# Statistics of x spread over fifteen steps, and three engines' programs unrolled twelve steps further

## The chip, the cores and the metric

The kernel runs on one core of a Trainium2 chip. The metric is the device time of one execution in microseconds (us). Engines: PE (TensorE: matmuls, with PEld for its weight loads), DVE (VectorE), ACT (ScalarE), POOL (GpSimd) and SP (SyncE), which here only issues DMAs. Each runs its own program in order; they meet at semaphores.

## The reference

One layer of cross attention and a mixture of experts behind it, 32 batches of 100 queries and 361 keys, width 256, 16 heads:

```
d  = layernorm(x)                                  # no gain, over 256 columns
q, k, v = d Wq + bq, ctx Wk + bk, ctx Wv + bv      # 16 heads of 16
z  = softmax(q k^T) v
x1 = x + layernorm(z + d) * gamma + beta
x2 = x1 + E(layernorm(x1)),  E(t) = t + sum over 2 of 8 experts of gate * ffn(layernorm(t))
```

What the change touches belongs to the first line: mean and variance of every row of x, from which come `rstd0` (one over the deviation) and `nb0` (minus the mean times it), one column for each batch.

## The kernel before

**Steps.** The attention is a software pipeline over the batches, one step for each, written as `iteration(turn, i)` for each engine. In step i, PE computes the row scores of batch i+1 (only for the row maxima, which DVE takes as `negmax`, L1390), the transposed scores of batch i, and the projections of batch i+3. Batches i-1, i-2 and i-3 are in the later stages: z is normalised, added and normalised again, and routed. A step has 12 slots (`s` in the code), and tables (`PLACE`, `START`, `TAIL`) say in which slot each operation stands. There are steps from -3 to 39; the experts' tiles follow and overlap with the last.

**Loops.** `pipeline(eng, iteration, first, last)` writes out the steps from -3 to 3*first-1, puts the steps from there to 26 into a loop of three steps a turn, and writes out the rest. PE and SP have `first=1`, so their loops begin at step 3; DVE, ACT and POOL have `first=2` and begin at step 6. In the loop a batch's number comes from a register; in written-out code it is a constant. What is special to one step (loads, statistics of x) can only stand in written-out code, behind `isinstance(turn, int)`.

**Statistics of x.** x is loaded in six parts, `X_LOADS`. Part 0 is issued by ACT, part 1 by SP at the start, part 2 by SP behind the first two key stacks, and parts 3, 4 and 5 (`X_LOAD_BEHIND`) by SP right behind the key stacks of batches 2, 3 and 4, that is in steps 0, 1 and 2. DVE takes a `bn_stats` for each batch (`x_sums`, L1330): batches 0 to 11 before step -1, and batches 12 to 31 five a step in steps 0 to 3, at the slots of `X_SUM_AT`. It waits for `x_loaded` at the first batch of each part. The sums are turned into deviations in four parts, `X_PARTS`: eight small operations on DVE (`x_variance_step`, L1340 to L1354), one a slot in slots 4 to 11 of steps 2 and 4 for the last two parts, then a power on POOL at the end of the same step (`inverse_deviation_x`, L694), and the offset on DVE at the end of the next (`x_offset`, L1363). ACT waits for `nb0_ready` before it normalises rows of a new part (steps 1 and 5, and in the loop).

**The key stack.** The keys of batch i+3 are split into three bfloat16 parts. ACT makes the high part and the middle one, POOL the rest (`k_rest`, L795) and the low part (`k_part`, L798, "the key part" below). SP waits for the low part and issues six DMAs of 192 KB (L660) that put the parts into `k_stack`, which lies in the tensor `stack_x`; PE's first row score of the batch, one step and some slots later, waits for them. Behind these SP issues a part of x where there is one, then the context of a later batch (`ct`, L635), then `zscr` (L645), by which z is laid out anew through DRAM; `z_in` (L639) reads it back, and POOL's `u` (L807) needs it. POOL's order in a step is: low part of the queries (L779), reciprocal deviation of the second norm (L788), `k_rest`, `u`, the key part, reciprocal deviation of the first norm (L810), and the rest.

**Guard.** `guard` (L1395) is DVE's cleaning of the exponentials `p_t`, four a step, at slots 0, 3, 6 and 9.

**Expert weights.** ACT issues 14 DMAs of 256 KB for `w1_s`, two in each turn of its loop, in the steps with i mod 3 of 0 and 1, at slot 5.

Of the kernel before, what the change touches and what calls it, by code (L numbers as in the profile page):

```python
# [12 lines left out]
B, Q, D = 32, 100, 256  # L13
# [14 lines left out]
FIRST = 4  # L28
X_LOADS = [slice(0, FIRST), slice(FIRST, 12), slice(12, 17), slice(17, 22), slice(22, 27), slice(27, B)]
X_LOAD_BEHIND = {1: 2, 2: 3, 3: 4, 4: 5}  # L30
X_SUM_AT = {(n // 5, (1, 4, 7, 9, 10)[n % 5]): 12 + n for n in range(20)}
TAIL_FROM = B - 3
X_PARTS = [slice(0, FIRST), slice(FIRST, 12), slice(12, 22), slice(22, B)]
SCORES_LAG, GUARD_LAG, VALUES_LAG = 3, 6, 9
# [112 lines left out]
def pipeline(eng, iteration, first=1, last=9):  # L147

    for i in range(-3, 3 * first):
        iteration(0, i)  # L150
    with eng.Fori(first, last) as turn:
        for r in range(3):
            iteration(turn, r)
    for i in range(3 * last, END):
        iteration(0, i)


def build(nc, x, ctx_t, wq_t, bq, wk_t, bk, wv_t, bv, gamma, beta, ln_g, ln_b, rw, rb, w1, b1, w2, b2,
          ident_d, route_c, zscr, zf_d, out):
    es = ExitStack()  # L160
    with es:
# [25 lines left out]
        w1_s = sb(es, "w1_s", [128, 2, E, HF])  # L187
# [277 lines left out]
        with att:  # L465
# [214 lines left out]
            def _(pool):  # L680
# [10 lines left out]
                def inverse_deviation_x(k):  # L691

                    pool.wait_ge(ln0_step, 8 * (k + 1))
                    g.tensor_tensor(rstd0[:, X_PARTS[k]], ln0[0][:, X_PARTS[k]], half[:, 0:1].broadcast_to([Q, X_PARTS[k].stop - X_PARTS[k].start]), ALU.pow).then_inc(rstd0_ready, 1)  # L694

# [60 lines left out]
                def iteration(turn, i):  # L756
# [7 lines left out]
                    for s in range(NG):  # L764
# [48 lines left out]
                        for k in tiles_at(turn, i, s):  # L813
                            tile_step(k)
                    if isinstance(turn, int) and i in (-2, 2, 4):
                        inverse_deviation_x({-2: 1, 2: 2, 4: 3}[i])

                pipeline(pool, iteration, first=2)
                pool.wait_ge(x2_late, 16 * (B - LOOSE))
# [281 lines left out]
            def _(act):  # L1101
# [118 lines left out]
                def iteration(turn, i):  # L1220
                    if isinstance(turn, int) and i == -2:
                        act.wait_ge(q_const, 48)
                        nc.scalar.activation(ident_bf[:], ident[0:Q, 0:Q], ACT.Copy).then_inc(ident_ready, 1)
                    if isinstance(turn, int) and i in (1, 5):
                        act.wait_ge(nb0_ready, {1: 2, 5: 3}[i])
                    if not isinstance(turn, int) and i == 0:
                        act.wait_ge(nb0_ready, len(X_PARTS))
                    if isinstance(turn, int) and i in WEIGHT_LOADS:
                        load_weights(i)
                    for s in range(NG):  # L1230
                        at = moment(turn, i, s)
                        for a in due(turn, i, s, 3, "ACT", "q"):
                            queries_high(a)
                        if not isinstance(turn, int) and i < 2 and s == 5:
                            act.dma_start(w1_s[:, i, bass.ds(turn - 2, 1), :].rearrange("p e f -> p (e f)"),
                                          w1[bass.ds(turn - 2, 1), i * 128:i * 128 + 128, :].rearrange("e p f -> p (e f)")).then_inc(w1_loaded, 16)
# [67 lines left out]

                pipeline(act, iteration, first=2)
                remaining(act, tile_step, LOOP[0])
# [3 lines left out]
            def _(dve):  # L1310
# [210 lines left out]
                def iteration(turn, i):  # L1521
                    for s in range(NG):
# [15 lines left out]
                        if isinstance(turn, int) and (i, s) in X_SUM_AT:  # L1538
# [4 lines left out]
                            x_sums(range(n, n + 1))  # L1543
                        if isinstance(turn, int) and i in (2, 4) and 4 <= s < 12:
                            x_variance_step({2: 2, 4: 3}[i], s - 4)
                        if isinstance(turn, int) and (i, s) == (-1, 0):
# [92 lines left out]
                    if isinstance(turn, int) and i == -2:  # L1639
                        dve.wait_ge(x_loaded[1], 16)  # L1640
                        x_sums(range(B)[X_LOADS[1]])
                        x_variance(1)
                    if isinstance(turn, int) and i in (-1, 3, 5):
                        x_offset({-1: 1, 3: 2, 5: 3}[i])

                pipeline(dve, iteration, first=2)
                remaining(dve, tile_step, LOOP[0])
# [63 lines left out]
```

## Time and profile before

| | us |
|---|---|
| median of 3 runs | 834.51 |
| lowest and highest | 834.42, 835.29 |
| the profiled execution, in all | 837.38 |
| its span, first to last instruction | 835.5 |
| PE busy | 752.3 (90%) |
| DVE busy | 629.9 (75%) |
| ACT busy | 564.1 (68%) |
| POOL busy | 536.1 (64%) |

The page has the busy time of each engine over the whole span. The table of stretches has the same for pieces of it, with the clock that was granted to TensorE as a share of 2.4 GHz. Here the cuts are the starts of PE's first row score of a batch: step 1 is 52.8 to 69.6, step 2 69.6 to 88.2, step 3 88.2 to 106.6, step 4 106.6 to 124.3, step 5 124.3 to 141.1, step 6 141.1 to 156.5, step 7 156.5 to 172.7, step 8 172.7 to 188.0, step 9 188.0 to 203.3, and steps 10 to 26 are 203.3 to 463.9. A line of waits tells who waited for whom, the total, how many times, and the longest. A line of a timeline has start and length in us, engine and line, the operation with its tiles as out<-in and their shapes, and in brackets the idle time of the engine before it and what ended it. Tiles go by the name of the tensor they lie in: x and the key stack are both `stack_x`, the q parts `q_part`.

### The profile page before, as it was taken

To read this page: it belongs to the slowest core of one execution; us is meant where nothing else is said; L and a number is where in the kernel's file an instruction comes from. 1 tells how busy PE (TensorE), PEld (TensorE's weight loads), DVE (VectorE), ACT (ScalarE), POOL (GpSimd) and SP (SyncE) were. 2 spreads that over 40 slices of the span, in tenths; PEclk is the share of its full clock that TensorE was granted. 3 is DMA by queue.
4 is the path that set the end of the run, shared out by engine and by line. 5 is a ranking of instruction groups with operands and counts; after the bars stand their busy time and mean duration, and the time that the engine had idled before them with its cause. 6 is when DMAs were issued, how large, how long until landed. Compare 5 with 4: busy or idle time off the path is not lost.

```text
span 835.5 us, 26294 instructions
## 1 busy us (share of the span) xinstructions
PE 752.3 (90%) x8080; PEld 587.7 (70%) x8081; DVE 629.9 (75%) x1781; ACT 564.1 (68%) x1469; POOL 536.1 (64%) x609
## 2 busy tenths in 40 slices
PE   7888989999999999999999997555979888999994
PEld 4565666767777777777777674435878777999994
DVE  7688998989989999989999897784366763445441
ACT  3466767878888888888888785334565544666662
POOL 5433657767768767777777674335656555777773
PEclk9999999999999999999999999755989998999998
DMA  8566665777786786877877868511334323443341
GB/s 216 145 142 163 151 149 125 176 167 153 163 180 153 172 173 148 184 151 165 180 152 164 193 126 206 165 21 43 61 56 59 58 40 58 70 70 58 62 66 18
DMA packets 154001, 104.43 MB, mean 125 GB/s; under 512 B 68365, under 2 KB 149561, under 8 KB 153817
## 3 DMA queue, kind: packets, MB, share of 16 engines
q1 hardware_dynamic: 135502, 79.47, 43.3%
q0 software_dynamic: 10944, 14.10, 10.6%
q10 hardware_dynamic: 7498, 10.18, 4.1%
q8 instruction: 28, 0.46, 0.2%
q14 instruction: 29, 0.23, 0.1%
HBM read 36.65 MB, written 17.33 MB: 65 GB/s over the span
## 4 chain that ended last, share of the span: by engine, by line
PE 58%; DMA 12%; DVE 9%; POOL 6%; issue 6%; SPq 5%; ACT 2%; DVEq 1%; ACTq 0%; POOLq 0%
PE s_row L1004 9%; PE pj L899 7%; PE s_row L913 7%; PE zt L945 6%; PE s_t L933 6%; PE pj L868 6%; PE pj L1015 4%; PE zt L1015 4%; SPq L660 3%; DMA out_x<-index_space,idx_s 3%; DVE negmax L1390 2%; DMA q_stack<-m_part 2%; PE pj L886 2%; DMA zscr<-zn 2%; DMA stack_x<-k_part 2%
## 5 line engine op out<-in xcount | busy, mean ns | idle before, releaser
L1390 DVE TENSOR_REDUCE negmax<-s_row 100x1 f32<-100x361 f32 x512 | 250.9, 522 | 23.6 <-PE s_row L913 19.3
L1209 ACT ACTIVATE p_t<-s_t 128x400 f32<-128x400 f32 x384 | 188.0, 499 | 82.1 <-PE s_t L933 74.3
L913 PE MATMUL s_row<-stack_x,q_stack 125*128 125x361 bf16 x512 | 132.5, 319 | 16.5 <-DVE negmax L1390 8.6
L730 POOL DMA_INDIRECT out_x<-index_space,idx_s x57 | 91.3, 1601 | 77.1 <-ACT index_space L1194 35.4
L933 PE MATMUL s_t<-q_stack,stack_x 128*128 128x100 bf16 x1536 | 129.4, 211 | 11.0 <-ACT p_t L1209 7.9
L933 PEld LDWEIGHTS s_t<-q_stack,stack_x 128*128 128x128 bf16 x1536 | 94.5, 99 | 56.1 <-issue 31.3
L1004 PE MATMUL s_row<-w_qkv,v_aug 128*128 128x128 f32 x912 | 117.9, 285 | 1.7 <-DVE v_aug L1485 1.7
L1004 PEld LDWEIGHTS s_row<-w_qkv,v_aug 128*128 128x128 f32 x912 | 113.2, 202 | 2.3 <-DVE v_aug L1485 2.2
L1395 DVE TENSOR_SCALAR p_t<-p_t 128x1200 f32<-128x1200 f32 x128 | 100.8, 787 | 11.4 <-ACT p_t L1209 11.3
L899 PE MATMUL pj<-w_qkv,ct 128*128 128x256 f32 x384 | 104.8, 395 | 0.3 <-ACT k_rest L1130 0.3
L945 PE MATMUL zt<-p_t,v_aug 128*32 128x100 f32 (+1 forms) x3072 | 96.3, 260 | 0.8 <-DVE p_t L1395 0.8
L945 PEld LDWEIGHTS zt<-p_t,v_aug 128*32 128x32 f32 (+1 forms) x3072 | 66.9, 113 | 32.9 <-issue 31.6
L868 PE MATMUL pj<-ct,w_qkv 128*128 128x361 f32 x248 | 89.2, 483 | 0.0
L1188 ACT ACTIVATE w_qkv<-s_row,b_k 128x128 f32<-128x128 f32 x228 | 64.9, 367 | 29.2 <-PE s_row L1004 29.0
L913 PEld LDWEIGHTS s_row<-stack_x,q_stack 125*128 125x128 bf16 x512 | 46.2, 101 | 52.0 <-DVE negmax L1390 41.0
L715 POOL DMA_INDIRECT q_part<-zf_d,idx_g x57 | 68.5, 1202 | 19.4 <-issue 15.9
L899 PEld LDWEIGHTS pj<-w_qkv,ct 128*128 128x128 f32 x384 | 65.6, 190 | 6.4 <-issue 0.6
L1180 ACT ACTIVATE w_qkv<-pj,lnb_c,lng_c 128x128 f32<-128x128 f32 x57 | 26.1, 457 | 51.4 <-PE pj L992 51.3
L1485 DVE TENSOR_SCALAR v_aug<-w_s 128x1024 f32 x57 | 40.7, 714 | 23.7 <-issue 22.7
L807 POOL TENSOR_TENSOR u<-z_in,td 100x256 f32<-100x256 f32 x32 | 43.1, 1347 | 21.5 <-DMA z_in<-zscr 20.4
L1015 PE MATMUL pj<-stack_x,w_qkv 128*128 x232 | 56.4, 387 | 0.0
L798 POOL TENSOR_TENSOR k_part<-k_rest,k_part 128x722 bf16<-128x722 f32 x32 | 50.2, 1568 | 7.2 <-ACT k_part L1139 7.1
(244 smaller groups left out, 1413.9 us busy)
## 6 DMA issues: line engine op xcount, KB each, us to landing
stack_x<-k_part SPq DMA_DIRECT2D x192, 192.0 KB, 3.6
q_stack<-q_part SPq DMA_DIRECT2D x192, 64.0 KB, 2.0
ct<-in_ctx_t SPq DMA_DIRECT2D x32, 361.0 KB, 4.3
stack_x<-in_w ACTq DMA_DIRECT2D x8, 512.0 KB, 6.4
w_s<-in_w ACTq DMA_DIRECT2D x14, 256.0 KB, 3.0
zscr<-zn SPq DMA_DIRECT2D x32, 100.0 KB
z_in<-zscr SPq DMA_DIRECT2D x32, 100.0 KB
zf_d<-zf_s SPq DMA_DIRECT2D x32, 100.0 KB
```

What stands on the lines that cost most here:

```text
L715: pool.indirect_dma_start(zg[:, k.ring, :], None, zf_rows[0:n], bass.IndirectOffsetOnAxis(idx_g[:, k.ring:k.ring + 1], 0), bounds_check=n ...
L730: pool.indirect_dma_start(out_rows[0:n], bass.IndirectOffsetOnAxis(idx_s[:, k.slot:k.slot + 1], 0), ys[:, k.slot, :], None, bounds_check=n ...
L868: last = nc.tensor.matmul(keys_bank(a, t)[:, 0:KEYS], wk_s[:, c, t * 128:t * 128 + 128], ct[:, a.slot, c, 0:KEYS], start=(c == 0), stop=(c ...
L899: last = nc.tensor.matmul(bank[:, kt % 2 * D:kt % 2 * D + D], ct[:, b.slot, c, kt * 128:kt * 128 + 128], wv_s[:, c, :], start=(c == 0), st ...
L913: nc.tensor.matmul(s_row[h % 2][:, 0:KEYS], q_stack[0:MROW, b.slot, h, :], k_stack[0:MROW, b.slot, h, 0:KEYS], start=True, stop=True).then ...
L933: last = nc.tensor.matmul(s_t[g % 2][:, j * Q:j * Q + Q], k_stack[:, b.slot, h, kt * 128:kt * 128 + 128], q_stack[:, b.slot, h, 0:Q], star ...
L945: last = nc.tensor.matmul(zt[32 * j:32 * j + 32, quad * Q:quad * Q + Q], v_aug[0:n, b.slot, kt * H + 4 * quad + j, :], p_t[0:n, quad % 2, ...
L1004: last = nc.tensor.matmul(p_h[k.slot][:, j * 128:j * 128 + 128], w1_k[k.slot][:, c * HF + j * 128:c * HF + j * 128 + 128], zgt[:, k.slot, ...
L1015: last = nc.tensor.matmul(p_y[k.slot][:, 0:D], hidt[:, k.slot, c * 128:c * 128 + 128], w2_s[:, bass.ds(e, 1), c, :].rearrange("p e f -> p ...
L1209: nc.scalar.activation(p_t[:, quad % 2, kt, :], s_t[g % 2][:, 0:4 * Q], ACT.Exp).then_inc(exp_done, 1)
L1390: v.tensor_reduce(negmax[:, b.slot, h:h + 1], s_row[h % 2][0:Q, 0:KEYS], AXIS.X, ALU.max, negate=True).then_inc(max_done, 1)
L1395: v.tensor_scalar(p_t[:, quad % 2], p_t[:, quad % 2], 0.0, None, ALU.max).then_inc(p_ready, 1)
```

## The change

The sums of batches 12 to 31 are spread out: one or two a step in steps 0 to 6 (two in step 0), two a step in steps 9 to 14. The last two variances stand in steps 7 and 15, their powers at the end of these, their offsets at the end of steps 8 and 16, and ACT's waits for the offsets at the start of steps 9 and 17. The last two parts are batches 12 to 19 and 20 to 31 rather than 12 to 21 and 22 to 31, and the last four loads hold 4, 4, 6 and 6 batches rather than 5 each, issued where they were. So that these steps can hold special operations, DVE, ACT and POOL have the steps up to 17 written out (`first=6`), and their loops run over 18 to 26. The first eight DMAs for the expert weights, which were in the loop, are written out at the same steps and slots.

```diff
--- before.py
+++ after.py
@@ -26,11 +26,13 @@
 NG = G * KT
 TINY = 1e-30
 FIRST = 4
-X_LOADS = [slice(0, FIRST), slice(FIRST, 12), slice(12, 17), slice(17, 22), slice(22, 27), slice(27, B)]
+X_LOADS = [slice(0, FIRST), slice(FIRST, 12), slice(12, 16), slice(16, 20), slice(20, 26), slice(26, B)]
 X_LOAD_BEHIND = {1: 2, 2: 3, 3: 4, 4: 5}
-X_SUM_AT = {(n // 5, (1, 4, 7, 9, 10)[n % 5]): 12 + n for n in range(20)}
+X_SUM_AT = {(0, 4): 12, (0, 9): 13, (1, 4): 14, (2, 4): 15, (3, 4): 16, (4, 4): 17, (5, 4): 18, (6, 4): 19}
+X_SUM_AT.update({(9 + n // 2, (4, 9)[n % 2]): 20 + n for n in range(12)})
+X_VARIANCE_AT = {7: 2, 15: 3}
 TAIL_FROM = B - 3
-X_PARTS = [slice(0, FIRST), slice(FIRST, 12), slice(12, 22), slice(22, B)]
+X_PARTS = [slice(0, FIRST), slice(FIRST, 12), slice(12, 20), slice(20, B)]
 SCORES_LAG, GUARD_LAG, VALUES_LAG = 3, 6, 9
 QPAD = 128
 NT = (2 * B * Q + E * 127) // 128
@@ -812,10 +814,10 @@
                             g.tensor_tensor(nb[:], nmean[:], rstd[:], ALU.mult).then_inc(nb_ready, 1)
                         for k in tiles_at(turn, i, s):
                             tile_step(k)
-                    if isinstance(turn, int) and i in (-2, 2, 4):
-                        inverse_deviation_x({-2: 1, 2: 2, 4: 3}[i])
-
-                pipeline(pool, iteration, first=2)
+                    if isinstance(turn, int) and i in (-2, 7, 15):
+                        inverse_deviation_x({-2: 1, 7: 2, 15: 3}[i])
+
+                pipeline(pool, iteration, first=6)
                 pool.wait_ge(x2_late, 16 * (B - LOOSE))
                 pool.reg_mov(gathers[0], NF + 5)
                 remaining(pool, tile_step, LOOP[0])
@@ -1221,16 +1223,16 @@
                     if isinstance(turn, int) and i == -2:
                         act.wait_ge(q_const, 48)
                         nc.scalar.activation(ident_bf[:], ident[0:Q, 0:Q], ACT.Copy).then_inc(ident_ready, 1)
-                    if isinstance(turn, int) and i in (1, 5):
-                        act.wait_ge(nb0_ready, {1: 2, 5: 3}[i])
-                    if not isinstance(turn, int) and i == 0:
-                        act.wait_ge(nb0_ready, len(X_PARTS))
+                    if isinstance(turn, int) and i in (1, 9, 17):
+                        act.wait_ge(nb0_ready, {1: 2, 9: 3, 17: 4}[i])
                     if isinstance(turn, int) and i in WEIGHT_LOADS:
                         load_weights(i)
                     for s in range(NG):
                         at = moment(turn, i, s)
                         for a in due(turn, i, s, 3, "ACT", "q"):
                             queries_high(a)
+                        if isinstance(turn, int) and 6 <= i < 18 and i % 3 < 2 and s == 5:
+                            act.dma_start(w1_s[:, i % 3, i // 3 - 2, :], w1[i // 3 - 2, i % 3 * 128:i % 3 * 128 + 128, :]).then_inc(w1_loaded, 16)
                         if not isinstance(turn, int) and i < 2 and s == 5:
                             act.dma_start(w1_s[:, i, bass.ds(turn - 2, 1), :].rearrange("p e f -> p (e f)"),
                                           w1[bass.ds(turn - 2, 1), i * 128:i * 128 + 128, :].rearrange("e p f -> p (e f)")).then_inc(w1_loaded, 16)
@@ -1302,7 +1304,7 @@
                         for k in tiles_at(turn, i, s):
                             tile_step(k)
 
-                pipeline(act, iteration, first=2)
+                pipeline(act, iteration, first=6)
                 remaining(act, tile_step, LOOP[0])
                 gated(Tile(0, NT - 1))
 
@@ -1541,8 +1543,8 @@
                                 if n == X_LOADS[k].start:
                                     dve.wait_ge(x_loaded[k], 16)
                             x_sums(range(n, n + 1))
-                        if isinstance(turn, int) and i in (2, 4) and 4 <= s < 12:
-                            x_variance_step({2: 2, 4: 3}[i], s - 4)
+                        if isinstance(turn, int) and i in X_VARIANCE_AT and 4 <= s < 12:
+                            x_variance_step(X_VARIANCE_AT[i], s - 4)
                         if isinstance(turn, int) and (i, s) == (-1, 0):
                             dve.wait_ge(route_const, 64)
                             for c in range(2):
@@ -1640,10 +1642,10 @@
                         dve.wait_ge(x_loaded[1], 16)
                         x_sums(range(B)[X_LOADS[1]])
                         x_variance(1)
-                    if isinstance(turn, int) and i in (-1, 3, 5):
-                        x_offset({-1: 1, 3: 2, 5: 3}[i])
-
-                pipeline(dve, iteration, first=2)
+                    if isinstance(turn, int) and i in (-1, 8, 16):
+                        x_offset({-1: 1, 8: 2, 16: 3}[i])
+
+                pipeline(dve, iteration, first=6)
                 remaining(dve, tile_step, LOOP[0])
                 result(Tile(0, NT - 1))
```

## Rows read from the trace of the kernel before

**Rows 1.** The page: busy time, share of the span and instructions of each engine.

```profile
PE 752.3 (90%) x8080; PEld 587.7 (70%) x8081; DVE 629.9 (75%) x1781; ACT 564.1 (68%) x1469; POOL 536.1 (64%) x609
```

**Rows 2.** Stretches: length, PE, PEld, DVE, ACT, POOL busy (count), clock, DMA share, GB/s.

```profile
52.80:69.60 16.80, 15.41 (x199) 10.87 (x198) 14.32 (x32) 11.22 (x30) 4.87 (x6) 1.00 0.56 137
69.60:88.20 18.60, 15.80 (x195) 10.85 (x196) 16.16 (x44) 11.71 (x30) 9.03 (x13) 1.00 0.72 159
88.20:106.60 18.40, 16.03 (x205) 11.32 (x202) 16.96 (x43) 13.11 (x34) 12.31 (x16) 1.00 0.66 143
106.60:124.30 17.70, 15.83 (x202) 11.46 (x203) 16.86 (x44) 13.00 (x33) 11.05 (x16) 1.00 0.67 142
124.30:141.10 16.80, 15.74 (x205) 11.24 (x201) 15.00 (x38) 13.03 (x34) 13.41 (x16) 1.00 0.58 137
...
156.50:172.70 16.20, 15.49 (x206) 11.26 (x205) 14.30 (x37) 13.44 (x34) 11.51 (x15) 1.00 0.78 166
...
203.30:463.90 260.60, 259.76 (x3421) 189.92 (x3420) 238.18 (x613) 222.45 (x562) 195.93 (x255) 1.00 0.75 165
```

**Rows 3.** Waits of DVE for x (total, times, longest), 38.5 to 40 and 53 to 57.

```profile
DVE stats L1330 <- DMA stack_x<-in_x: 0.7, 1, 0.7
...
DVE stats L1330 <- DMA stack_x<-in_x: 1.6, 1, 1.6
```

**Rows 4.** Timeline of POOL: start, length, operation, [idle before it <- what ended it].

```profile
77.25 0.72 POOL L807 TENSOR_TENSOR u<-z_in,td 100x256 f32<-100x256 f32 x1 [4.32 <-DMA z_in<-zscr]
77.94 1.56 POOL L798 TENSOR_TENSOR k_part<-k_rest,k_part 128x722 bf16<-128x722 f32 x1
...
96.22 1.57 POOL L798 TENSOR_TENSOR k_part<-k_rest,k_part 128x722 bf16<-128x722 f32 x1
```

**Rows 5.** SP's DMA issues in step 1, and the DMA packets of 66.3 to 75.1.

```profile
66.34 0.52 SPq L597 DMA_DIRECT2D stack_x<-in_x  x1
67.64 0.53 SPq L645 DMA_DIRECT2D zscr<-zn  x1
...
DMA packets 2724, 1.39 MB, mean 158 GB/s; under 512 B 1723, under 2 KB 2722, under 8 KB 2722
```

**Rows 6.** Timelines of DVE and POOL in step 4, then in step 9.

```profile
111.95 2.21 DVE L1340 TENSOR_TENSOR ln<-stats 100x10 f32<-100x10 f32 x1
...
112.58 1.56 POOL L798 TENSOR_TENSOR k_part<-k_rest,k_part 128x722 bf16<-128x722 f32 x1
...
192.61 0.77 DVE L1395 TENSOR_SCALAR p_t<-p_t 128x1200 f32<-128x1200 f32 x1
...
193.93 1.57 POOL L798 TENSOR_TENSOR k_part<-k_rest,k_part 128x722 bf16<-128x722 f32 x1
```

**Rows 7.** Timeline of DVE in step 2: a statistic, and the variance's first operation.

```profile
75.67 0.42 DVE L1330 BATCH_NORM_STATS2 stats<-stack_x 100x6 f32<-100x256 f32 x1
76.00 0.15 DVE L1340 TENSOR_TENSOR ln<-stats 100x10 f32<-100x10 f32 x1
```

**Rows 8.** Waits of PE for the key stack in step 5, then in step 7.

```profile
PE s_row L913 <- DMA stack_x<-k_part: 1.0, 1, 1.0
...
PE s_row L913 <- DMA stack_x<-k_part: 0.7, 1, 0.7
```

**Rows 9.** Timeline of POOL: powers of 8 and 10 columns; the key part of step 5.

```profile
24.93 1.64 POOL L694 TENSOR_TENSOR rstd<-ln,half 100x8 f32<-100x8 f32 x1
...
124.01 2.49 POOL L694 TENSOR_TENSOR rstd<-ln,half 100x10 f32<-100x10 f32 x1 [0.50 <-DVE ln L1354]
...
130.81 1.58 POOL L798 TENSOR_TENSOR k_part<-k_rest,k_part 128x722 bf16<-128x722 f32 x1
```

**Rows 10.** DMA queues (packets, MB, share): 0 to 141.1; 164 to 168.2; 188 to 463.9.

```profile
q14 instruction: 8, 0.06, 0.1%
...
q14 instruction: 1, 0.01, 0.8%
...
q10 hardware_dynamic: 1728, 3.15, 4.4%
```

## The prediction

> **What bounds the kernel now.** I read the page first, then a table of stretches cut where TensorE starts the first row score of a batch (one stretch is one step), then the waits and timelines where a step is longer than the others. The page has PE busy for 90% of the span [rows 1]; the table says why that is not the whole answer [rows 2]. From step 10 to step 26 the 17 steps take 260.6 us, 15.33 each, with PE busy for 259.8 of it: PE is the bound there, with DVE at 238.2/17 = 14.0 a step, some 1.3 us below. Steps 1 to 5 take 16.8, 18.6, 18.4, 17.7 and 16.8 us, 11.7 us above five such steps, and step 7 takes 16.2. The granted clock is 1.00 (2.4 GHz) in all of them, so none of this is the clock. The change works on these steps, so the question is what ends last in each.
>
> In steps 0 and 1 it is DVE: it stands in front of a statistic until that part of x has landed, 0.7 and 1.6 us [rows 3], and row maxima and PE's row scores queue behind it. In steps 2 and 3 it is not DVE, though DVE is busiest there. POOL waits 4.32 us for z_in and only then makes u and the lowest key part, which ends at 79.50, then 97.79 [rows 4]: 18.3 us apart, the step's own length. I read this as a ring through the DMA queue: key parts into the stack, then the load of x that SP issues behind them, then the context, then z out [rows 5], z in, u, the next key part. All of it is on SP's queue, and 1.39 MB pass at 158 GB/s before z is out. Step 4 is DVE's: busy 16.9 of 17.7 us [rows 2]. One tiny operation, the first of the variance's eight, takes 2.21 us [rows 6] where the same line took 0.15 in step 2 [rows 7]. It ends at 114.16, and POOL's key part at 114.14 [rows 6]. Step 5 ends in a wait of 1.0 us for the key stack and step 7 in one of 0.7 [rows 8].
>
> **The change part by part.** *Statistics and loads, steps 0 to 6.* Twenty statistics at some 0.33 us each (75.67 to 76.00, the start of the next operation [rows 7]) leave steps 0 to 3; eight come back one or two a step in 0 to 6. The waits for x go, since each sum now comes a step or more after its load: 0.7 in step 0, 1.6 in step 1.
> - Step 0: the wait of 0.7, and the statistic behind it, 0.3, of which I take a part: 0.8 (0.7 to 1.0).
> - Step 1: 1.6 + 0.33 x 2 = 2.2 is on offer, but the step can't fall below PE's 15.33, from 16.8: 1.3. Total 2.1.
> - Steps 2 and 3: the ring. The loads are 4, 4, 6 and 6 batches where they were 5 each; the last two go out in steps 1 and 2, ahead of z. 100 KB more at 158 GB/s [rows 5] is 0.65 us in each turn of the ring. Key part 3 is 2.1 earlier, so part 4 is 1.5 and part 5 0.9 earlier; whatever DVE saves beyond that, PE waits for the key stack instead. Total gain at the end of step 3: 1.0 (PE's first score of step 4 hangs on that landing).
> - Step 4: no variance and no load. From 17.7 down to about 15.8, as key part 5 is only 0.9 ahead and the ring has to catch up with PE: total 2.9.
> - Step 5: POOL's power of ten columns (2.49 us, [rows 9]) is gone ahead of it. With it the key part began 6.5 us into the step (130.81), without it 5.9 in a steady one (193.93 after 188.0) [rows 6, 9]: 0.6. Total 3.5.
> The bounds of this term: 1.5, if the ring is slowed more by the larger loads, and 12.5, if the ring follows DVE and all of the 11.7 + 0.8 goes.
>
> *Variances, steps 7 and 15.* They stand at slots 4 to 11 as before, the first right behind the guard of p_t. In step 4 it starts 5.4 us into the step and POOL's key part 6.0 (111.95, 112.58 after 106.6). In step 9, a steady one that begins at 188.0, the guard ends at 5.4 (192.61 + 0.77) and the key part starts at 5.9 [rows 6]. So the operation should meet u and the key part again and stand for 2.1 us. Eight at 0.15 are 1.2 more at most. 3.3 less the 1.3 that DVE has spare is 2.0; step 4 as a whole says 17.7 - 15.3 = 2.4, with later small collisions in it. I take 2.4, twice: +4.8. The bounds for each are 0 (no collision, and 1.2 fits under the spare) and 3.3.
>
> *POOL's powers, end of steps 7 and 15.* Eight columns took 1.64, ten 2.49 [rows 9]; twelve I estimate at 2.9 from the two. POOL is idle for (260.6 - 195.9)/17 = 3.8 us of a steady step [rows 2], in pieces, and ten put the key part back by 0.6. So eight are taken as hidden: 0 (bound 0.5), and twelve as 0.6 + 0.4 = 1.0, of which slack before PE's first score hides a little: +0.8 (0 to 1.5). Behind it on POOL stand q_low, k_rest, u and the key part.
>
> *Statistics, steps 9 to 14.* Two a step, 0.67 of DVE's spare 1.3. That of slot 9 has no row maximum in its slot. That of slot 4 comes ahead of two, which PE needs two scores later. I take 0.05 a step: +0.3 (0 to 0.3 x 6 = 2.0).
>
> *Waits that move.* ACT's waits for the offsets move to steps 9 and 17, one slot behind DVE's offsets, as the loop's first wait stood before; nothing queues there: 0. The weight loads of steps 6 to 16 keep their slots and sizes: 0, as long as ACT isn't late.
>
> *Unrolling.* In the loop there is next to nothing to gain: 260.6 - 259.8 = 0.8 us of PE idle in 17 steps [rows 2]; four turns fewer on three engines can give 0.6 at most, and I take 0. What it adds is code to fetch, and fetches share the DMA engines. Queue 14 shows 8 packets of 8 KB by 141.1 and one at 164 to 168; over the loop, 188 to 464, the list ends with queue 10 and has no instruction queue [rows 10]. The packet at 164 to 168 lies in step 7, while the key stack is under way, and step 7 is the one that waits 0.7 and lasts 16.2 [rows 2, 8]. At about one packet a step I expect ten more in steps 6 to 17. The transfer fills half a step, so five fall into it; I take 0.3 each, a mean of none and 0.7: +1.5. Bounds: -0.9, if step 7's excess goes as well and no packet hurts, and +5.
>
> The Trainium skill (Runtime: NRT & Kernel Launch, "Instruction fetch mechanics") speaks against this term twice: it calls the cost of crossing into the next block "mostly hidden", and says that taken branches break the prefetch, a reason to unroll. By the first the sum would lose its 1.5, by the second up to 0.6 more. It has blocks of 16 KiB, where queue 14 shows packets of 8 KB. On the second the trace does not agree: a loop whose 17 steps hold 0.8 us of PE idle has no stall worth the name. On the first it is open.
>
> **Sum.** -3.5 + 4.8 + 0 + 0.8 + 0.3 + 1.5 = +3.9 us. The profiled execution took 837.38 us with a span of 835.5, 1.9 around it; after the change I expect a span near 839.4 and 841.3 in all. The median of the runs is 2.9 below that execution, and 834.51 + 3.9 = 838.4.
>
> **The rivals.**
> - *DVE was the bound all along (faster).* The place is steps 1 to 5. If z is sent early enough when DVE and PE run ahead, the ring shortens with them and all 12.5 us go. Against 7.4 that come later this gives -5.1, 829.4. For it: DVE's 16.2 to 17.0 busy us in steps 2 to 4. Against: POOL's 4.32 us for z_in and SP's order. It turns the sign once the start gives more than 7.4. Chance 0.18.
> - *The collision doesn't come back (no change).* In steps 7 and 15 POOL's u or key part comes a little later, the 2.1 us don't appear, and DVE's spare takes the rest: 3.9 - 4.4 = -0.5, 834.0. For it: in step 2 the first operation took 0.15 only, since POOL was late. Against: the equal spacing in steps 4 and 9. Chance 0.17.
> - *Fetches hurt more.* Every packet in a transfer costs the 0.7 of step 7, and some delay z or the maxima too: +3.5 more, 842. Chance 0.1.
> - *Unrolling pays and fetching is free.* Code arrives ahead of use without holding up a transfer, and the turns that are gone gave the 0.6: 838.4 - 2.1 = 836.3. For it: no engine is seen to stand for code. Against: step 7. Chance 0.07, about half on either side of the border. (It is what the Trainium skill's page on the runtime, Runtime: NRT & Kernel Launch, would have.)
>
> **How the numbers follow.** The forecast has 0.48. A measurement here can tell about 0.2%, 1.7 us. Slower by more: 0.48 + 0.1 + 0.04 = 0.62; within: 0.17 + 0.03 = 0.20; faster: 0.18. The range leaves out the far part of the fast rival and of the costly fetches: 831.5 to 842.5. The likeliest case alone spans 836 to 841.
>
> **What would show it.** Steps 0 and 1 without a DVE wait for x, near 15.3; step 3 not shorter than before, with POOL waiting for z_in and PE for the key stack; steps 7 and 15 near 17.7 with a first variance operation of about 2 us; step 8 as its neighbours, step 16 near 16.1; some packets on the instruction queue in steps 9 to 17, and longer steps where they meet the key transfer. I am wrong if steps 2 and 3 fall below 17 us, or if steps 7 and 15 stay at 15.4.

## The result, and the profile after

The changed kernel takes 843.70 us (median of 20 runs, 839.32 to 848.16) where the kernel before takes 835.85 beside it (20 runs): a ratio of 1.0089, 95% interval 1.0073 to 1.0104. It is slower by 7.4 us by the ratio and by 7.9 between the medians; 3.9 were forecast, and the range ended at 842.5. The profiled execution took 843.64 us, with a span of 841.6 where it was 835.5.

The stretches of the changed kernel, cut again where PE starts a batch's first row score: steps 1, 2, 3, 4, 7, then 9 to 14 together, 15 and 16. The columns are those of [rows 2].

```profile
53.00:68.70 15.70, 15.16 (x196) 10.81 (x197) 13.25 (x27) 11.25 (x29) 5.75 (x6) 1.00 0.55 136
68.70:87.60 18.90, 15.27 (x196) 10.77 (x197) 14.29 (x32) 11.85 (x30) 10.46 (x12) 1.00 0.71 157
87.60:107.00 19.40, 15.64 (x202) 11.33 (x203) 14.50 (x37) 13.07 (x33) 10.77 (x15) 1.00 0.68 144
107.00:122.80 15.80, 15.63 (x202) 11.26 (x203) 14.35 (x37) 13.08 (x33) 11.36 (x15) 1.00 0.66 150
154.40:173.00 18.60, 16.97 (x202) 12.70 (x203) 17.09 (x45) 13.34 (x34) 11.32 (x16) 0.91 0.72 155
188.20:281.40 93.20, 92.94 (x1211) 67.53 (x1210) 88.32 (x229) 78.06 (x199) 63.16 (x90) 1.00 0.74 164
281.40:301.50 20.10, 18.55 (x200) 13.70 (x201) 17.01 (x44) 13.08 (x33) 11.53 (x16) 0.83 0.66 144
301.50:316.80 15.30, 15.30 (x205) 11.19 (x204) 13.94 (x38) 12.91 (x34) 12.90 (x16) 1.00 0.65 152
```

Against [rows 2]: step 1 has lost 1.1 us and step 4 1.9. Steps 2 and 3 are longer, 18.9 and 19.4 where they were 18.6 and 18.4, though DVE's busy time in them fell from 16.2 and 17.0 to 14.3 and 14.5. Steps 9 to 14 take 93.2/6 = 15.53 instead of 15.33. Steps 7 and 15 are the long ones, 18.6 and 20.1, with a mean clock of 0.91 and 0.83.

POOL's timeline in steps 2 and 3, the answer to [rows 4]:

```profile
76.79 0.73 POOL L809 TENSOR_TENSOR u<-z_in,td 100x256 f32<-100x256 f32 x1 [4.82 <-DMA z_in<-zscr]
77.48 1.56 POOL L800 TENSOR_TENSOR k_part<-k_rest,k_part 128x722 bf16<-128x722 f32 x1
...
96.01 0.72 POOL L809 TENSOR_TENSOR u<-z_in,td 100x256 f32<-100x256 f32 x1 [4.10 <-DMA z_in<-zscr]
96.69 1.57 POOL L800 TENSOR_TENSOR k_part<-k_rest,k_part 128x722 bf16<-128x722 f32 x1
```

POOL waits 4.82 us for z_in in step 2 (4.32 before) and 4.10 in step 3 (1.73 before). The key parts end at 79.04 and 98.26, 19.2 us apart where they were 18.3.

What PE stood for in steps 2 and 3 together, first before, then after (total, times, longest):

```profile
PE s_row L913 <- DVE negmax L1390: 1.9, 3, 1.2
PE s_t L933 <- DMA q_stack<-m_part: 1.6, 2, 1.0
...
PE s_t L935 <- DMA q_stack<-m_part: 4.2, 2, 2.4
PE s_row L915 <- DMA stack_x<-k_part: 2.3, 2, 1.2
```

The longest waits are no longer for DVE but for `m_part`, the row maxima, which SP sends to `q_stack` on the same queue behind the load of x, the context and `zscr`. The stack of keys comes second.

The collision of [rows 6], found again in step 7 and in step 15 (first the variance's first operation on DVE, then POOL's key part):

```profile
159.70 2.22 DVE L1342 TENSOR_TENSOR ln<-stats 100x8 f32<-100x8 f32 x1
...
160.34 1.56 POOL L800 TENSOR_TENSOR k_part<-k_rest,k_part 128x722 bf16<-128x722 f32 x1
...
286.71 2.22 DVE L1342 TENSOR_TENSOR ln<-stats 100x12 f32<-100x12 f32 x1
...
287.34 1.56 POOL L800 TENSOR_TENSOR k_part<-k_rest,k_part 128x722 bf16<-128x722 f32 x1
```

The operation takes 2.22 us both times and ends with POOL's key part, at 161.92 beside 161.90 and at 288.93 beside 288.90. PE's row score in step 7, and the stretch of half clock behind it:

```profile
162.42 0.77 PE L915 MATMUL s_row<-stack_x,q_stack 125*128 125x361 bf16 x2 [1.52 <-DVE negmax L1392]
...
164.60:168.00 3.40, 3.40 (x20) 3.09 (x19) 2.77 (x8) 2.90 (x9) 3.15 (x5) 0.50 1.10 231
```

PE stood 1.52 us for DVE's maxima, just as in step 4 of the kernel before (1.51 at 114.67, its timeline says). But here the granted clock falls to 0.50 (1.2 GHz) at 164.6 for 3.4 us, and in step 15 at 290.9 for 6.8. POOL's powers, of 8 and of 12 columns, and the instruction queue between 188 and 470:

```profile
172.32 2.18 POOL L696 TENSOR_TENSOR rstd<-ln,half 100x8 f32<-100x8 f32 x1 [0.30 <-DVE ln L1356]
...
300.56 2.28 POOL L696 TENSOR_TENSOR rstd<-ln,half 100x12 f32<-100x12 f32 x1
```

```profile
q14 instruction: 12, 0.10, 0.1%
```

Here the power of twelve takes 2.28 us where 2.9 was worked out. But this is the execution with half clock ahead of it; in the other four profiles of the changed kernel it takes 2.80 or 2.81, as in this one:

```profile
299.14 2.81 POOL L696 TENSOR_TENSOR rstd<-ln,half 100x12 f32<-100x12 f32 x1 [0.50 <-DVE ln L1356]
```

Queue 14 has 12 packets where the list of [rows 10] had none.

### The profile page after: what moved, and what is told of

It is laid out like the page before. It is cut to its first block, busy times and chain, and to the rows that moved or that the text cites. A ratio compares the mean times of both kernels' runs of the same rounds, so it can differ in the third digit from the quotient of the medians.

```text
span 841.6 us, 25567 instructions
## 1 busy us (share of the span) xinstructions
PE 754.4 (90%) x8080; PEld 589.4 (70%) x8081; DVE 631.6 (75%) x1781; ACT 564.9 (67%) x1469; POOL 532.3 (63%) x609
## 4 chain that ended last, share of the span: by engine, by line
PE 62%; DMA 9%; DVE 9%; SPq 6%; issue 5%; POOL 5%; ACT 2%; DVEq 1%; ACTq 0%; POOLq 0%
PE s_row L1006 10%; PE pj L901 8%; PE s_row L915 7%; PE zt L947 6%; PE s_t L935 6%; PE pj L870 6%; PE pj L1017 5%; PE zt L1017 4%; SPq L662 3%; DMA zscr<-zn 3%; PE pj L888 3%; DVE negmax L1392 2%; DMA z_in<-zscr 2%; PE pj L994 1%; DMA q_stack<-m_part 1%
## 5 line engine op out<-in xcount | busy, mean ns | idle before, releaser
L915 PE MATMUL s_row<-stack_x,q_stack 125*128 125x361 bf16 x512 | 134.3, 323 | 16.4 <-DVE negmax L1392 8.0
L732 POOL DMA_INDIRECT out_x<-index_space,idx_s x57 | 92.4, 1621 | 74.2 <-ACT index_space L1196 34.9
L717 POOL DMA_INDIRECT q_part<-zf_d,idx_g x57 | 69.0, 1211 | 20.0 <-issue 15.6
L781 POOL TENSOR_TENSOR q_part<-q_rest,q_part 128x200 bf16<-128x200 f32 x32 | 18.1, 566 | 58.4 <-ACT q_part L1137 58.4
```

Of the source, the lines that this page charges most:

```text
L717: pool.indirect_dma_start(zg[:, k.ring, :], None, zf_rows[0:n], bass.IndirectOffsetOnAxis(idx_g[:, k.ring:k.ring + 1], 0), bounds_check=n ...
L732: pool.indirect_dma_start(out_rows[0:n], bass.IndirectOffsetOnAxis(idx_s[:, k.slot:k.slot + 1], 0), ys[:, k.slot, :], None, bounds_check=n ...
L915: nc.tensor.matmul(s_row[h % 2][:, 0:KEYS], q_stack[0:MROW, b.slot, h, :], k_stack[0:MROW, b.slot, h, 0:KEYS], start=True, stop=True).then ...
```

## The experiments

Two theories stood against each other. The first is the prediction's own: the ring, the moved variances and a little for code. The second is that the written-out programs themselves cost the time. Kernels that were timed together shared their runs of the kernel before. Where a label has a ratio, it was timed; the others are single profiled executions, below called profiles.

**Unrolling alone** (`unroll_only`). The kernel before, with this:

```diff
-                pipeline(dve, iteration, first=2)
+                pipeline(dve, iteration, first=6)
...
+                        if isinstance(turn, int) and 6 <= i < 18 and i % 3 < 2 and s == 5:
+                            act.dma_start(w1_s[:, i % 3, i // 3 - 2, :], w1[i // 3 - 2, i % 3 * 128:i % 3 * 128 + 128, :]).then_inc(w1_loaded, 16)
```

ACT and POOL likewise, and ACT's wait for the last offsets in step 6.

> The kernel before with only the unrolling (DVE, ACT and POOL written out up to step 17, the expert weights' DMAs with them); statistics, variances and loads of x as before. Theory 1 (the moved variances and the ring are the cost, code is cheap): -0.5 to +2 us against before, with some nine more packets on the instruction queue in steps 6 to 17, and steps 9 to 17 within 0.1 us of 15.33 except where a packet meets the key transfer (0.2 to 0.4 longer). Theory 2 (code fetching or the written-out programs themselves are the cost): +4 to +7 us, spread over steps 6 to 17.

Measured: ratio 1.0015 (0.9992 to 1.0037). Its steps 6 and 7, and the instruction queue from 188 to 309.6:

```profile
140.80:156.20 15.40, 15.40 (x202) 11.19 (x203) 13.86 (x36) 12.83 (x33) 11.38 (x15) 1.00 0.70 167
156.20:171.50 15.30, 15.30 (x206) 11.19 (x203) 14.03 (x37) 13.04 (x34) 11.50 (x15) 1.00 0.77 172
...
q14 instruction: 7, 0.06, 0.2%
```

There are packets, 7 in that stretch, and DVE, ACT and POOL run from written-out code, yet step 7 is 15.3 long, shorter than before, and steps 9 to 14 take 92.2 us where they took 92.0. Theory 2, which asked for 4 us and more, has fallen. So has my term of 1.5 us for the fetches: the long step 7 of the kernel before went away with its packet, and the new ones cost 0.2 us in six steps. All of the 0.2 is in step 14, which has a packet 8 and one 11 us into it and lasts 15.5 to 15.6 us. That a packet can lengthen a step is thus borne out; that most of them do isn't.

**The variances at another place** (`late_slots`). The changed kernel with

```diff
-                        if isinstance(turn, int) and i in X_VARIANCE_AT and 4 <= s < 12:
-                            x_variance_step(X_VARIANCE_AT[i], s - 4)
+                        if isinstance(turn, int) and i in X_VARIANCE_AT and s >= 10:
+                            for n in range(4 * (s - 10), 4 * (s - 10) + 4):
+                                x_variance_step(X_VARIANCE_AT[i], n)
```

> The changed kernel with the eight operations of each of the last two variances at slots 10 and 11, four in each, in place of one a slot from slot 4 on; there POOL is mostly idle. Theory 1: the first operation stands for well under 0.5 us instead of 2.2; PE is not kept idle, the granted clock stays at 1.00 in steps 7 and 15, both last 15.5 to 16.2 us instead of 18.6 and 20.1, and the time is 6 to 7 us under the changed kernel's (ratio to before 0.998 to 1.003). Theory 2: the steps keep most of their length, under 2 us gained.

**The changed kernel again** (`after_again`), timed together with `late_slots`.

> The changed kernel once more, for the spread between executions. If the half clock in steps 7 and 15 follows from the collision, it is there again (one stretch or two of 3.4 us in each); if it was chance, one or both steps show a clock of 1.00 and last some 17 us. The first variance operation stands for 2.2 us in either case. Ratio to before 1.007 to 1.010.

Measured: ratios 1.0028 (1.0003 to 1.0052) and 1.0069 (1.0043 to 1.0094). The second profile of the changed kernel has this in steps 7, 8, 15 and 16:

```profile
155.60:173.20 17.60, 15.75 (x203) 11.38 (x202) 16.93 (x45) 13.11 (x34) 11.10 (x16) 1.00 0.78 163
173.20:188.70 15.50, 15.50 (x206) 11.33 (x204) 14.59 (x38) 12.97 (x34) 13.13 (x16) 1.00 0.57 136
281.70:299.40 17.70, 15.90 (x201) 11.41 (x202) 16.85 (x44) 12.98 (x33) 10.97 (x16) 1.00 0.75 161
299.40:315.40 16.00, 15.60 (x205) 11.24 (x202) 15.10 (x38) 12.84 (x34) 13.75 (x16) 1.00 0.61 148
```

and with the variances moved the same four steps are

```profile
154.90:170.20 15.30, 15.30 (x202) 11.18 (x202) 14.18 (x43) 12.90 (x34) 11.48 (x15) 1.00 0.76 170
170.20:186.40 16.20, 16.02 (x206) 11.27 (x203) 15.41 (x40) 13.20 (x34) 13.34 (x16) 1.00 0.68 146
280.00:295.30 15.30, 15.30 (x201) 11.10 (x202) 14.12 (x41) 12.78 (x33) 11.45 (x15) 1.00 0.73 168
295.30:312.00 16.70, 15.92 (x205) 11.24 (x204) 15.88 (x41) 13.03 (x34) 13.95 (x16) 1.00 0.68 156
```

Steps 7 and 15 of the changed kernel are 17.6 and 17.7 when the clock stays at 1.00, which is the length forecast, and their first operation took 2.21 and 2.22 us here too. The half clock is not a fixed part of them. Without the collision both are at 15.3, with all eight operations in them. Of the 4.7 us so gained, steps 8 and 16 give 1.4 back. There POOL waits 1.19 us for DVE's last operation before its power, which I read as the cause: the power begins later against PE than it did. I had expected 6 to 7 us in the timing, from the profile with the half clock; it was 837.84 against 841.19, 3.4.

**Loads of five** (`loads_of_five`).

```diff
-X_LOADS = [slice(0, FIRST), slice(FIRST, 12), slice(12, 16), slice(16, 20), slice(20, 26), slice(26, B)]
+X_LOADS = [slice(0, FIRST), slice(FIRST, 12), slice(12, 17), slice(17, 22), slice(22, 27), slice(27, B)]
```

> The changed kernel with the last four loads of x holding five batches each, as before the change, the sums staying where they are. If the ring through the DMA queue binds steps 2 and 3 and each load of x ahead of z costs its transfer time, steps 2 and 3 are 0.6 shorter each (18.9 and 19.4 to about 18.3 and 18.6) and PE starts step 4 at about 105.7 instead of 107.0. If the sizes don't matter, step 4 starts at 107.0 still.

Measured: ratio 1.0041 (1.0016 to 1.0066), step 4 starts at 105.8. Steps 2 and 3:

```profile
68.40:87.00 18.60, 15.28 (x195) 10.78 (x195) 14.29 (x32) 11.85 (x31) 10.47 (x12) 1.00 0.72 160
87.00:105.80 18.80, 15.64 (x202) 11.33 (x203) 14.50 (x37) 13.04 (x33) 10.76 (x15) 1.00 0.64 140
```

Together 37.4, instead of 38.3 in the first profile of the changed kernel and 38.7 on the mean of five: the larger loads cost 0.9 to 1.2 us, where 1.3 was worked out. With the loads of before and DVE's busy time 4 us lower in the two steps, they are as long as in the kernel before (37.3 on the mean).

**The loads out of the ring** (`pieces`). The changed kernel, with batches 20 to 31 as six loads of two, one in each of steps 3 to 8, behind z_in on SP's queue (SP's program is written out up to step 8 for it):

```diff
+X_LOAD_IN_STEP = {3: 4, 4: 5, 5: 6, 6: 7, 7: 8, 8: 9}
...
                             sp.dma_start(z_in[:, d.slot], rows).then_inc(z_loaded[d.slot], 16)
+                            if isinstance(turn, int) and i in X_LOAD_IN_STEP:
+                                x_load(X_LOAD_IN_STEP[i])
```

> The changed kernel with the loads of batches 20 to 31 taken out of steps 1 and 2 and issued as six loads of two batches right behind z_in in steps 3 to 8 (SP's program written out up to step 8). If the ring through the DMA queue is what binds steps 2 and 3, they fall from 18.9 and 19.4 to 15.5 to 16.5 us each, POOL's wait for z_in goes, and PE starts step 4 at 100 to 102 instead of 107.0; the later steps keep their lengths. If DVE or the start of the normalisation binds them, they stay above 17.5.

Measured: ratio 1.0004 (0.9986 to 1.0022), step 4 starts at 100.6. Steps 2 and 3, and POOL's wait for z_in in step 2:

```profile
68.60:84.70 16.10, 15.36 (x199) 10.77 (x195) 14.22 (x33) 12.05 (x31) 10.98 (x12) 1.00 0.67 143
84.70:100.60 15.90, 15.84 (x202) 11.29 (x203) 14.56 (x37) 13.02 (x33) 10.75 (x15) 1.00 0.61 148
...
73.33 1.25 POOL L812 TENSOR_TENSOR u<-z_in,td 100x256 f32<-100x256 f32 x1 [1.43 <-DMA z_in<-zscr]
```

The two steps fall from 38.3 to 32.0 us while DVE's work in them is the same. It was the loads on SP's queue that bound them. POOL's wait is 1.43 us where it was 4.82, and PE's waits for `m_part`, 1.84 and 2.41 us, are gone. Which of the two transfers, z or the maxima, set the length isn't told apart by this run, since the loads stood ahead of both.

**Both** (`pieces_late`): the loads in pieces and the variances at slots 10 and 11.

> As the run with the loads in pieces, with the variances at slots 10 and 11 as well. The two gains add: some 5 to 6 us under the run with the late variances alone, so 832 to 833 where the kernel before has 835 (ratio 0.994 to 0.998). If they don't add, another wait has taken over in steps 7, 8, 15 or 16.

Measured: 830.36 us, ratio 0.9929 (0.9911 to 0.9947), a little under the 0.994 to 0.998 expected. Together they gain at least what they gain singly (the changed kernel has 1.0089, or 1.0069 the second time), and this version beats both kernels.

**The statistics off slot 4** (`sums_late`).

```diff
-X_SUM_AT = {(0, 4): 12, (0, 9): 13, (1, 4): 14, (2, 4): 15, (3, 4): 16, (4, 4): 17, (5, 4): 18, (6, 4): 19}
-X_SUM_AT.update({(9 + n // 2, (4, 9)[n % 2]): 20 + n for n in range(12)})
+X_SUM_AT = {(0, 9): 12, (0, 10): 13, (1, 9): 14, (2, 9): 15, (3, 9): 16, (4, 9): 17, (5, 9): 18, (6, 9): 19}
+X_SUM_AT.update({(9 + n // 2, (9, 10)[n % 2]): 20 + n for n in range(12)})
```

> The changed kernel with the statistics that stand at slot 4 moved to slots 9 and 10, where no row maximum stands. If it is the place ahead of two row maxima that costs time, steps 9 to 14 fall from 15.5 to 15.3 or 15.4 and steps 4 to 6 from 15.8 to about 15.5: 2 us in all against the changed kernel. If it is DVE's load as such, nothing changes.

Measured: ratio 1.0067 (1.0050 to 1.0084), no difference that the timing can tell. In the profile steps 5 and 6, then steps 9 to 14:

```profile
124.40:155.90 31.50, 31.05 (x403) 22.53 (x404) 28.69 (x74) 25.85 (x66) 20.39 (x30) 1.00 0.72 161
188.90:281.30 92.40, 92.15 (x1211) 67.19 (x1209) 87.79 (x229) 77.76 (x199) 62.76 (x90) 1.00 0.75 166
```

Steps 9 to 14 fall from 93.2 to 92.4 (15.40 each), so two thirds of their excess hung on slot 4. Steps 4, 5 and 6 are 15.7, 16.0 and 15.5, together 47.1 against 47.4 on the mean: that part of the expectation was wrong, and what holds steps 4 and 5 is not the statistic.

**Short powers** (`parts_of_four`): pieces as above, the statistics at slots 9 and 10 of steps 0 to 15, and five variances of four batches.

```diff
-X_VARIANCE_AT = {7: 2, 15: 3}
+X_VARIANCE_AT = {4: 2, 7: 3, 10: 4, 13: 5, 16: 6}
-X_PARTS = [slice(0, FIRST), slice(FIRST, 12), slice(12, 20), slice(20, B)]
+X_PARTS = [slice(0, FIRST), slice(FIRST, 12)] + [slice(n, n + 4) for n in range(12, B, 4)]
```

> Loads in pieces as above; the statistics one a step at slot 9 (now and then one at slot 10) in steps 0 to 15, and the last twenty batches' variances in five parts of four batches, in steps 4, 7, 10, 13 and 16, at slots 10 and 11, with five short powers on POOL. If POOL's power of 8 to 12 columns is what makes steps 8 and 16 long (16.2 and 16.7), powers of four columns fit into POOL's idle time there and no step from 4 to 17 is over 15.6: ratio to before 0.989 to 0.993. If the place at the end of the step is what hurts, the steps after 4, 7, 10, 13 and 16 each last 0.5 longer.

Measured: 830.01 us, ratio 0.9926 (0.9906 to 0.9946), level with `pieces_late`. Steps 7 and 8, and the power at the end of step 7:

```profile
146.20:161.50 15.30, 15.26 (x201) 11.16 (x202) 14.15 (x41) 12.83 (x33) 10.50 (x15) 1.00 0.76 182
161.50:177.50 16.00, 15.63 (x204) 11.15 (x203) 15.40 (x44) 13.05 (x34) 12.01 (x16) 1.00 0.71 161
...
162.23 1.50 POOL L698 TENSOR_TENSOR rstd<-ln,half 100x4 f32<-100x4 f32 x1 [1.60 <-DVE ln L1360]
```

Step 7 has the variance and is short; step 8, behind the power, is 16.0. A power of four columns is no cheap one: it takes 1.50 us here. The steps behind the other four are 16.3, 16.0, 16.2 and 16.0; step 6, which has none ahead of it, is 16.3 too, and that stays open. Four columns behind step 7 cost as much as eight did, which speaks for the place, between the maxima and the next step's queries and keys; no run has the power elsewhere. Five short powers gained nothing over two long ones.

**More profiles.** The parts above account for some 4 of 7 us, so the kernels before and after and the one with the unrolling alone were profiled more often.

> The kernel before once more, for a second look at its steps. [...]

> [...] The start up to PE's first score of step 1 is expected at 52 to 53 us, and 1 to 2 later where the half clock around 20 us lasts 6.8 instead of 3.4 us.

> The changed kernel a third time. If the half clock in steps 3, 7 and 15 comes by chance behind PE's waits, about half of the looks have one or more of them; steps 7 and 15 last 17.7 without and 18.6 to 20.2 with. Between the first row score of step 1 and that of step 27 it takes 3.5 to 4 us more than the kernel before without any, 6 with all.

> The changed kernel a fourth time, for the spread: as in the third look, steps 7 and 15 at 17.7 us without half clock and at 18.6 to 20.2 with it, steps 2 and 3 at 18.9 and 19.4 us within 0.4.

> The kernel before, a fourth look. If the clock around 20 us is chance, about half of all looks have half clock there and the first row score of step 0 comes at 36.0 us without, 37.4 with 3.4 us of it and 39.0 with 6.8. If it belongs to the new schedule, this one has 36.0 to 37.4.

> The kernel with the unrolling alone, a second look. If longer programs bring the half clock around 20 us and the longer end, it starts step 0 at 37.4 to 39.0 us and has 323 us behind step 30; if they don't, 36.0 and 321 to 322.

> The kernel with the unrolling alone, a third look: step 0 starts at 37.4 to 39.0 us if longer programs bring the half clock around 20 us, at 36.0 if they don't. Steps 9 to 14 take 91.9 to 92.3 us in either case.

> The changed kernel, a fifth look. If the half clock around 20 us belongs to the new schedule, step 0 starts at 37.3 to 39.2 us as in the four looks so far; if it was chance, 36.0 is as likely. Steps 1 to 26 take 414.5 to 417.1 us.

Mean lengths in us, from the starts of PE's first row scores in the timelines (4, 3 and 5 profiles, the profiled executions of the results among them):

| stretch | before | unrolling alone | after | after - before |
|---|---|---|---|---|
| up to step 0 | 36.6 | 37.0 | 38.4 | +1.9 |
| step 0 | 15.7 | 15.9 | 15.2 | -0.5 |
| step 1 | 16.8 | 17.2 | 15.6 | -1.2 |
| steps 2, 3 | 37.3 | 37.1 | 38.7 | +1.4 |
| steps 4 to 6 | 49.8 | 49.9 | 47.4 | -2.4 |
| steps 7, 8 | 31.5 | 30.6 | 33.2 | +1.7 |
| steps 9 to 14 | 92.0 | 92.2 | 93.3 | +1.4 |
| steps 15, 16 | 30.7 | 30.7 | 34.1 | +3.4 |
| steps 17 to 26 | 153.2 | 153.4 | 153.2 | 0.0 |
| steps 27 to 29 | 47.8 | 48.0 | 47.9 | 0.0 |
| from step 30 on | 321.2 | 322.0 | 322.9 | +1.7 |
| span | 832.5 | 833.9 | 839.9 | +7.3 |

Within a stretch of steps 1 to 26 the profiles of one kernel lie within 1.0 us of one another, but for the half clock of the first profile after. Single steps vary more: steps 2 and 3 are 19.3 and 17.6 in `before_again`, where the clock was at 0.50 for 3.4 us from 80.2, and 18.6 and 18.4 in the first profile before. Two entries stay open, the first and the last but one. The change leaves the tail alone, and the opening too, but for a load of x at 33 us that holds four batches instead of five.

Up to step 0 the kernels before took 36.0 to 37.4 us and the changed one 37.3 to 39.3. Three of its five profiles have 6.8 us of half clock at 20 to 21 us, where before and the unrolling alone have 3.4 or none. But `parts_of_four`, with the same opening and a new schedule, has none and starts step 0 at 36.0; over all profiles 6.8 us of it were seen in 5 of 11 with the new schedule and in 0 of 7 without. That may be chance. Over these 18 profiles step 0 starts at 35.9 to 37.8 us without half clock ahead of it, at 37.3 to 37.6 with 3.4 us, and at 38.7 to 39.3 with 6.8. From the means of the three groups (36.6, 37.5, 39.0) I estimate that 1.4 of the 1.9 us go with the clock; why the changed kernel had more of it isn't shown.

From step 30 on the profiles spread from 319.4 to 323.6 before and from 321.2 to 324.0 after, so 1.7 us is hardly more than that spread. Here too more half clock goes with a longer tail: leaving out the last 15 us, the two tails with 65 us of it take 319.4 and 320.5, the four with 75 us 322.9 to 324.0. But on the mean the changed kernel has only 1.7 us more (71.7 against 70.0), and a line through the 18 gives 0.5 us for that, as an estimate. The unrolling alone has 0.4 us more than the kernel before at the start and 0.8 more from step 30 on, and nothing in steps 0 to 26. That agrees with its 1.1 us in the timing, but its ratio can't be told from 1. I found no cause for the rest.

## Why the prediction was right in its parts and wrong in its size

- **Steps 0 and 1: right.** 0.8 and 1.3 forecast, 0.5 and 1.2 measured. (In step 2 of the kernel before DVE also stood 1.0 us for x, a wait that the prediction leaves out; nothing came of it, since the queue bound that step.)
- **Steps 2 and 3: the queue right, the wait only in part.** It was said that they would not shorten and that the larger loads would lengthen each turn by 0.65. Together they are 1.4 longer; 1.1 longer had been forecast (a gain of 2.1 at their start, 1.0 at their end). `pieces` shows that the loads on the queue are the cause. But the prediction had PE wait for the key stack, at the end of the ring through z. PE waits for it, by 1.1 and 1.2 us in the first profile, and longer, by 1.8 and 2.4, for the row maxima (1.8 to 2.6 in all five). Their transfer stands behind the same loads and isn't in the prediction's ring.
- **Steps 4 to 6:** 2.5 forecast (1.9 and 0.6), 2.4 measured.
- **Steps 7, 8, 15, 16: right.** Measured from 15.33 a step, the collisions and the powers were to cost 4.8 + 0.8 = 5.6; the means are 33.2 + 34.1 - 61.3 = 6.0, and 5.4 in the four profiles in which the clock stayed at 1.00 in them (33.0 and 33.7). 17.7 for the steps with a variance and 16.1 for step 16 came out as written. The part for twelve columns was right in its working too: 2.9 us estimated, 2.80 or 2.81 in those four.
- **Half clock in them: missed.** The text had the clock at 1.00 and asked no further. It adds 0.9 us to step 7 and 2.5 to step 15 in one of five profiles. The step behind is 0.7 shorter there, so that 0.5 is left on the mean of the five.
- **Statistics in steps 9 to 14: mis-sized.** 0.05 a step taken, 0.2 measured (with the packets of step 14 in it), inside the bound of 0.3.
- **Fetching: wrong.** 1.5 taken; the kernel with the unrolling alone gives -0.9 in steps 7 and 8 and +0.2 in steps 9 to 14. In all four profiles of the kernel before a packet lies some 10 us into step 7, which lasts 16.1 to 16.2 us. The reading of it in [rows 10] made a rule of one packet. The Trainium skill's "mostly hidden" (Runtime: NRT & Kernel Launch, "Instruction fetch mechanics") is what the run shows, and its reason to unroll isn't: nothing measurable was gained either.

So over steps 0 to 26 the sum stands: 3.9 forecast, 3.8 on the mean of the profiles (-0.5 - 1.2 + 1.4 - 2.4 + 1.7 + 1.4 + 3.4). That it is so near is in part luck, since the errors for the fetches, the statistics and the clock stand against each other. The step that failed is the one before the total: it carried +3.9 over to the whole execution as if the rest stood still. The start and the end differ by 3.5 us between the profiles, almost half of the result; most of the start's share goes with the granted clock, and what lies behind that and behind the end isn't known. To this comes the base. 838.4 was worked out from 834.51, the median of three runs, and the twenty have 835.85: 1.3 of the 5.3 us by which the time was missed are the base, 4.0 the change. The range had no room for either: starts of one kernel differ by up to 1.9 us between its profiles and its tails by up to 4.1, and 843.70 lies 1.2 above the upper end.

## What to carry to other kernels

A step that looks bound by the busiest engine may be bound by a ring of small waits through a DMA queue. Follow what the late engine waits for and what lies ahead of it in that queue: here taking 12 batches of loads out of it gave 6.3 us, and relieving DVE by 2 us a step gave none. List every small transfer behind the large one, not only the first that is found. When small operations are moved, ask beside which POOL instruction each will fall; the same eight operations cost 2.4 us more a step from slot 4 on than at slots 10 and 11, though the steps behind gave 1.4 of the 4.7 back. Profile a kernel several times before a sum of a few us is compared with a difference of a few us, and measure the base as often as the change.

## What the runs showed of the hardware

- A DVE operation with two inputs in SBUF, which took 0.15 us in step 2 of the kernel before, took 2.21 to 2.23 in each of the ten such steps (7 and 15) of the five profiles after: it began while POOL's `u` ran and ended with the key part behind it. In one of the four profiles of the kernel before, POOL's key part came later in step 4 (113.54, after the operation at 113.26); there it took 0.17, and PE didn't stand. The Trainium skill (SBUF — State Buffer, "SBUF: two separate sides") says that one of the two holds the port pair for its whole instruction and the other blocks. The trace agrees, and adds that POOL's next instruction can go ahead of the waiting DVE.
- PE stood 1.5 us in step 7 and 1.4 in step 15 in all five profiles after, and in `loads_of_five`, `sums_late` and `pieces`. In two of the eight the granted clock then fell to 0.50 (1.2 GHz) in step 7, for 3.4 us each (the first profile after, and `loads_of_five`, whose step 7 lasts 18.8 us), and in the first also in step 15, for 6.8. PE stood as long in step 4 in three of the four profiles before and in the three of the unrolling alone, and the clock didn't fall behind any of these. In steps 2 and 3 of the five profiles after it stood ten times for 1.8 to 2.6 us for the row maxima, and the clock fell within 1.5 us of the end of four of these stands. A stand of 1.4 to 2.6 us may or may not cost clock.
- POOL's power took 1.04 us for 4 columns and 1.64 to 1.70 for 8 in the opening (9.9 and 24.5 us in `after_again`), but 1.50 for 4, 2.12 to 2.21 for 8, 2.49 for 10 and 2.75 to 2.81 for 12 at the steps' ends and starts, with the 2.28 of the first profile after as the one exception. At either place a column more takes some 0.15 to 0.18 us, and the place is worth 0.5. What makes the difference between the places isn't shown.
